# Mixture-of-experts routing: the map of tiles to tokens in bf16 parts, and two pieces of weight splitting moved to GpSimd

## The reference, cut to what matters

```python
logits = x @ w_gate                                # x: 2048 x 256
logits = SOFTCAP * jnp.tanh(logits / SOFTCAP)
probs = jax.nn.softmax(logits, axis=-1)
_, idx = jax.lax.top_k(probs, TOPK)                # TOPK = 2, E = 8
mask = jax.nn.one_hot(idx, E, dtype=probs.dtype).sum(-2)
weights = probs * mask
out = jnp.zeros_like(x)
for e in range(E):
    h = jax.nn.silu(x @ w1[e]) * (x @ w3[e])       # 256 x 512 each
    out = out + h @ w2[e] * weights[:, e:e + 1]    # 512 x 256
return out.reshape(orig_shape)
```

## Time and profile before

| | us |
|---|---|
| median of 3 runs | 1409.47 |
| lowest and highest run | 1405.94, 1411.13 |
| profiled execution, whole | 1412.31 |
| its span, first to last instruction | 1410.6 |

### The profile page before, as it was taken

The page is one execution under the profiler, slowest core; times in us unless marked ns, Lnnn a source line. Parts: engine busy times, 40 slices in busy tenths (PEclk is TensorE's granted clock), DMA queues, the critical chain, the costliest instruction groups (busy, mean ns, idle before and its releaser), DMA issues. The chain is left out here.

```text
span 1410.6 us, 28961 instructions
## 1 busy us (share of the span) xinstructions
PE 1322.5 (94%) x8611; PEld 1103.6 (78%) x8611; DVE 1084.0 (77%) x2711; ACT 955.8 (68%) x3247; POOL 917.4 (65%) x1109
## 2 busy tenths in 40 slices
PE   9999988897799999999999999999999978999991
PEld 4445666664599999999999999999999856899891
DVE  4899768896688888888888888888889856444443
ACT  3997457775488888888888878878778845323321
POOL 3996237774278787787887767767767824455542
PEclk9999999997999999999999999999999998999996
DMA  9421110000102002012020020010100257677764
GB/s 343 156 109 71 36 46 2 1 2 1 60 1 91 1 1 91 1 39 72 24 104 7 2 91 1 32 60 2 46 1 31 76 208 262 144 165 164 169 153 134
DMA packets 55164, 105.89 MB, mean 75 GB/s; under 512 B 5052, under 2 KB 33668, under 8 KB 52708
## 3 DMA queue, kind: packets, MB, share of 16 engines
q1 hardware_dynamic: 46100, 84.90, 17.5%
q0 software_dynamic: 7488, 10.23, 4.6%
q10 hardware_dynamic: 1424, 8.91, 1.5%
HBM read 75.58 MB, written 28.44 MB: 74 GB/s over the span
## 5 line engine op out<-in xcount | busy, mean ns | idle before, releaser
L1937 ACT ACTIVATE pr_<-ps,neg_ 128x128 f32<-128x128 f32 x512 | 181.0, 366 | 64.1 <-DVE neg_ L2131 64.1
L2024 POOL TENSOR_TENSOR rstd<-var,half 128x6 f32<-128x6 f32 x128 | 172.5, 1347 | 10.0
L1963 ACT ACTIVATE y<-ps,invsm 128x128 bf16<-128x128 f32 x512 | 146.2, 373 | 42.0 <-PE ps L1842 25.9
L2035 POOL TENSOR_TENSOR z<-t,m 128x512 fp32r<-128x512 bf16 x128 | 148.7, 1162 | 4.9 <-DVE t L2157 4.9
L1812 PE MATMUL ps<-qkt 128*128 128x128 f32 x1024 | 138.3, 278 | 2.2 <-ACT qkt L1929 2.1
L1853 PE MATMUL ps<-phi,z 128*128 128x256 f32 x512 | 138.1, 303 | 1.0 <-POOL z L2035 1.0
L2019 POOL TENSOR_TENSOR var<-stat,deps 128x6 f32<-128x6 f32 x128 | 26.1, 204 | 171.1 <-DVE stat L2096 171.0
L1812 PEld LDWEIGHTS ps<-qkt 128*128 128x128 f32 x1024 | 129.0, 191 | 6.9 <-ACT qkt L1921 2.7
L2028 POOL TENSOR_TENSOR pr_<-pr_,rec_ 128x512 f32<-128x512 f32 x128 | 132.8, 1038 | 2.0 <-DVE rec_ L2138 2.0
L1853 PE MATMUL ps<-plo,z 128*128 128x256 f32 x512 | 127.6, 280 | 0.0
L2613 POOL DMA_INDIRECT sums<-f_ys,f_ids x39 | 61.8, 1583 | 91.6 <-DMA sums<-f_ys,f_ids 74.8
(11 more groups left out here) (374 smaller groups left out, 4240.9 us busy)
## 6 DMA issues: line engine op xcount, KB each, us to landing
f_w_low<-w_low SPq DMA_DIRECT2D x39, 512.0 KB, 3.8
centred<-raw_weights ACTq DMA_DIRECT2D x8, 1024.0 KB, 3.9
w_low<-w_dram SPq DMA_DIRECT2D x8, 1024.0 KB, 11.7
aw_st<-centred SPq DMA_DIRECT2D x7, 1024.0 KB, 6.3
raw_weights<-wself_dram SPq DMA_DIRECT2D x4, 1024.0 KB, 13.8
raw_weights<-wcross_dram SPq DMA_DIRECT2D x4, 1024.0 KB, 14.5
w_rest<-w_dram SPq DMA_DIRECT2D x8, 512.0 KB, 4.0
w_high<-w_top SPq DMA_DIRECT2D x8, 512.0 KB, 2.7
```

The source lines that it names most:

```text
L1937: ins = act.activation(pr[:, u.par, h, :], bS[:, h * S:(h + 1) * S], ACT.Exp, bias=neg[:, u.par, h:h + 1], accum_out=tot[:, u.par, h:h + 1])
L1963: ins = act.activation(y[:, u.par, h * S:(h + 1) * S], bO[:, h * S:(h + 1) * S], ACT.Copy, scale=invsm[:, head:head + 1])
L2024: pool.tensor_tensor(rstd[:, u.par, 0:6], v, half[:, :], ALU.pow).then_inc(s_rstd, 1)
L2035: pool.tensor_tensor(z[:, u.par, :], t[:, u.par, :], m[:, u.par, :], ALU.subtract).then_inc(s_z, 1)
```

## The change

1. **The map in bf16.** Tile numbers, lane numbers, `at_tile` and `at_lane` are bf16, in which these small whole numbers are exact. The token's number is split: `first` (128 times the tile of tokens less 2048) and `behind` (partition less lane). `ids_of` holds both as 2 x 39 columns. VectorE makes `at_tile` for all 32 pairs in one operation and its product with `first` in another; GpSimd makes the product with `behind`, in 4 parts. All inputs lie in SBUF now.
2. **The shares in a second map.** Each share is cut into three bf16 parts that add up to it exactly (four small operations on GpSimd). VectorE multiplies them with `at_tile` (3 x 39 columns, 8 pairs at a time) behind `ids`, and 32 further TensorE products add them up in another bank. VectorE sums the three results to `weight`.
3. **The pieces.** TensorE subtracts pieces 0, 2, 4 and 5 (before 0, 2, 3 and 7), the banks of piece 4 between the groups of the map, those of piece 5 around the second map. GpSimd subtracts pieces 1 and 3 (`split_low_by_pool`), VectorE 6 and 7 (before 1, 4, 5 and 6). ScalarE alternates `split_high` and `keep` in halves.
4. **Waits.** The first gather waits for `ids` alone. The loads of `f_w_low` wait also for the second map.

```diff
-WARM_UNITS, WARM_PRODUCTS, WARM_AT_END, BY_PE = 4, (3, 4), 15, (0, 2, 3, 7)
+WARM_UNITS, WARM_PRODUCTS, WARM_AT_END, BY_PE = 4, (3, 4), 15, (0, 2, 4, 5)
+BY_POOL = (1, 3)
...
+    def split_low_by_pool(self, pool, q):
+        i, e = self.place(q)
+        pool.wait_ge(self.s_hi, q + 1)
+        pool.tensor_tensor(self.low[:, i, e, :], self.low[:, i, e, :].bitcast(F32),
+                           self.high[:, i, e, :].bitcast(F32), ALU.subtract).then_inc(self.s_lo_pool, 1)
...
                 sp.wait_ge(s_own, 1)
-                sp.wait_ge(s_ids, 2)
+                sp.wait_ge(s_ids, 1)
+                sp.wait_ge(s_shares_map, CHUNKS)
...
                 subtract(2)
...
+                for c in range(CHUNKS):
+                    map_ids(c)
+                    if c < CHUNKS - 1:
+                        subtract(4, range(c, c + 1))
+                subtract(4, range(CHUNKS - 1, PIECE * CB))
+                subtract(5, range(0, 2))
+                map_shares(0)
+                map_shares(1)
+                subtract(5, range(2, PIECE * CB))
+                map_shares(2)
+                map_shares(3)
...
                 experts.split_high(act, 1)
-                keep(0)
+                keep(0, early)
                 experts.split_high(act, 2)
+                keep(0, late)
                 experts.split_high(act, 3)
-                keep(2)
-                for q in range(4, UP_PIECES):
-                    experts.split_high(act, q)
-                keep(3)
-                keep(7)
+                keep(2, early)
+                experts.split_high(act, 4)
+                keep(2, late)
+                experts.split_high(act, 5)
+                keep(4)
+                experts.split_high(act, 6)
+                keep(5, early)
+                experts.split_high(act, 7)
+                keep(5, late)
...
+                experts.split_low_by_pool(pool, 1)
+                pool.wait_ge(s_mask, 1)
+                pool.tensor_copy(part[:, :, :, 0], best[:, :, :]).then_inc(s_part, 1)
+                pool.wait_ge(s_part, 1)
+                pool.tensor_tensor(rest[:, :, :], best[:, :, :], part[:, :, :, 0], ALU.subtract).then_inc(s_part, 1)
...
+                experts.split_low_by_pool(pool, 3)
+                pool.wait_ge(s_at_tile, 1)
+                pool.wait_ge(s_behind, 1)
+                for c in range(CHUNKS):
+                    pool.tensor_tensor(ids_of[:, c, :, 1, :], at_tile[:, c, :, :], across(behind, c, NT), ALU.mult
+                                       ).then_inc(s_behind_ids, 1)
...
+                dve.tensor_tensor(pairs(at_tile), tile_row[:, :].unsqueeze(1).to_broadcast([P, 2 * B, NT]), each(tile_code, NT),
+                                  ALU.is_equal).then_inc(s_at_tile, 1)
+                dve.wait_ge(s_at_tile, 1)
+                dve.wait_ge(s_first, 1)
+                dve.tensor_tensor(ids_of[:, :, :, 0, :].rearrange("p c n t -> p (c n) t"), pairs(at_tile), each(first, NT), ALU.mult
+                                  ).then_inc(s_first_ids, 1)
...
+                for c in range(CHUNKS):
+                    dve.tensor_tensor(at_lane[:, c, :, :], lane_row[:, :].unsqueeze(1).to_broadcast([P, CHUNK, P]),
+                                      across(lane_code, c, P), ALU.is_equal).then_inc(s_pairs, 1)
+                dve.wait_ge(s_map, CHUNKS)
+                link(dve.tensor_scalar(weight[:, :], ids_ps[:, 0:NT], empty[:, 0:1], None, ALU.add))
+                dve.tensor_tensor(ids[:, :], ids_ps[:, NT:2 * NT], weight[:, :], ALU.add).then_inc(s_ids, 1)
+                dve.wait_ge(s_part, 4)
...
+                share(0)
+                share(1)
+                owner_of_tiles()
                 experts.split_low(dve, 6)
+                share(2)
+                share(3)
+                experts.split_low(dve, 7)
```

More of the change, by code:

```diff
@@ L2331, in moe_layer @@
         tile_of = sbuf(ctx, "f_tile_of", [P, 2, B], F32)
-        lane_of = sbuf(ctx, "f_lane_of", [P, 2, B], F32)
-        token = sbuf(ctx, "f_token", [P, 2, B], F32)
-        token_i = sbuf(ctx, "f_token_i", [P, B], I32)
+        tile_code, lane_code, behind = (sbuf(ctx, "f_" + n, [P, 2, B], BF16) for n in ("tile_code", "lane_code", "behind"))
+        first_i, first = sbuf(ctx, "f_first_i", [P, 2, B], I32), sbuf(ctx, "f_first", [P, 2, B], BF16)
+        place_i, place = sbuf(ctx, "f_place_i", [P, 1], I32), sbuf(ctx, "f_place", [P, 1], F32)
+        rest = sbuf(ctx, "f_rest", [P, 2, B], F32)
+        part = sbuf(ctx, "f_part", [P, 2, B, 3], BF16)
         minus = sbuf(ctx, "f_minus", [P, P], F32R)
@@ L2344, in moe_layer @@
         (s_xh, s_cst, s_token, s_th, s_d, s_ex, s_mask, s_cnt, s_own, s_pairs, s_map, s_ids, s_xt, s_xe, s_up, s_si, s_mu, s_ht,
-         s_he, s_y, s_ye, s_go, s_minus, s_diff, s_left, s_link, s_at_tile, s_values) = (sem("f_" + n) for n in (
+         s_he, s_y, s_ye, s_go, s_minus, s_diff, s_left, s_link, s_at_tile, s_first, s_behind, s_behind_ids, s_first_ids, s_part, s_shares, s_shares_map) = (sem("f_" + n) for n in (
              "xh", "cst", "token", "th", "d", "ex", "mask", "cnt", "own", "pairs", "map", "ids", "xt", "xe", "up", "si", "mu",
-             "ht", "he", "y", "ye", "go", "minus", "diff", "left", "link", "at_tile", "values"))
+             "ht", "he", "y", "ye", "go", "minus", "diff", "left", "link", "at_tile", "first", "behind", "behind_ids", "first_ids", "part", "shares", "shares_map"))
         stats = sbuf(ctx, "f_stats", [P, B, 6], F32)
@@ L2424, in _, with subtract @@
             def _(pe):
-                def subtract(q):
+                def subtract(q, banks=range(PIECE * CB)):
                     pe.wait_ge(experts.s_hi, q + 1)
-                    for at, (i, e, c) in chunks(q):
+                    for at, (i, e, c) in chunks(q)[banks.start:banks.stop]:
                         if at >= len(turns):
@@ L2661, in _ @@
                 dve.wait_ge(s_mask, 1)
[L2662 to L2665 removed]
+                dve.wait_ge(s_token, 2)
+                dve.tensor_copy(first[:, :, :], first_i[:, :, :]).then_inc(s_first, 1)
+                link(dve.tensor_copy(place[:, :], place_i[:, :]))
+                link(dve.tensor_scalar(empty[:, :], place[:, :], float(TOK), None, ALU.add))
                 dve.wait_ge(s_cnt, 1)
@@ L2698, in _ @@
-                dve.wait_ge(s_values, 4 * B // CHUNK)
-                experts.split_low(dve, 1)
-                dve.wait_ge(s_map, 2 * B // CHUNK)
-                dve.tensor_scalar(ids[:, :], bH[:, 0:NT], empty[:, 0:1], None, ALU.add).then_inc(s_ids, 1)
-                dve.tensor_copy(weight[:, :], bH[:, NT:2 * NT]).then_inc(s_ids, 1)
-                link(dve.tensor_tensor(past[:, :, :], tile_no[:, :].unsqueeze(2).to_broadcast([P, NT + 1, E]),
-                                       end[:, :].unsqueeze(1).to_broadcast([P, NT + 1, E]), ALU.is_gt))
@@ L2705, in _ @@
-                link(dve.tensor_reduce(owner[:, :], past[:, :, :], AX.X, ALU.add))
-                dve.tensor_scalar(owners[:, :], owner[:, :], float(E - 1), None, ALU.min).then_inc(s_own, 1)
-                experts.split_low(dve, 4)
-                experts.split_low(dve, 5)
-                experts.split_low(dve, 6)
-                dve.wait_ge(s_ids, 2)
+                link(dve.tensor_scalar(tile_code[:, :, :], tile_of[:, :, :], -WHOLE, None, ALU.add))
+                link(dve.scalar_tensor_tensor(lane_code[:, :, :], tile_code[:, :, :], -float(P), row[:, :, :], ALU.mult, ALU.add))
@@ new lines, in _, with owner_of_tiles @@
+                dve.tensor_scalar(behind[:, :, :], lane_code[:, :, :], -1.0, place[:, 0:1], ALU.mult, ALU.add).then_inc(s_behind, 1)
+                def owner_of_tiles():
+                    link(dve.tensor_tensor(past[:, :, :], tile_no[:, :].unsqueeze(2).to_broadcast([P, NT + 1, E]),
+                                           end[:, :].unsqueeze(1).to_broadcast([P, NT + 1, E]), ALU.is_gt))
+                    link(dve.tensor_reduce(owner[:, :], past[:, :, :], AX.X, ALU.add))
+                    dve.tensor_scalar(owners[:, :], owner[:, :], float(E - 1), None, ALU.min).then_inc(s_own, 1)
@@ new lines, in _, with share @@
+                dve.wait_ge(s_part, 4)
+                def share(c):
+                    if c >= 2:
+                        dve.wait_ge(s_shares_map, c - 1)
+                    dve.tensor_tensor(shares[:, c % 2, :, :, :], at_tile[:, c, :, :].unsqueeze(2).to_broadcast([P, CHUNK, 3, NT]),
+                                      part[:, c // 2, c % 2 * CHUNK:c % 2 * CHUNK + CHUNK, :].unsqueeze(3).to_broadcast([P, CHUNK, 3, NT]),
+                                      ALU.mult).then_inc(s_shares, 1)
@@ L2712, in low_x @@
+                dve.wait_ge(s_ids, 1)
                 def low_x(u):
```

91 lines of the change are left out of this document (47 added, 44 removed).

## The result

The changed kernel takes 1418.95 us in the median of four runs (1418.74 to 1420.67), the kernel before beside it 1407.70 (1405.30 to 1411.13). The ratio is 1.0078, with a 95% interval of 1.0054 to 1.0101: slower by some 11 us. The forecast was 1417.5 us. The profiled execution of the changed kernel took 1420.67 us with a span of 1418.8, the one of before 1412.31 with 1410.6: 8.2 us between the spans, where the prediction's sum was 8.0. As the experiments show, that agreement is partly luck.

The account below looks back on a forecast made before the run. The prediction saw a race to the first up product between TensorE's queue and VectorE's routing. 8.6 + 2.8 - 3.3 + 0.3 - 0.4 = +8.0 us on the median 1409.47 gave 1417.5 us, 8-in-10 range 1406 to 1424.

Parts of the forecast that it names:

- Part 1: Routing on VectorE: two GpSimd pieces of up weights hold it at the shared port, +4.1 and +4.5, sum 8.6 us.
- the second small operation for the ids: Between the map and the first up product: one more small operation for ids, +0.3 us.
- rival B: VectorE's map and share operations: stall is there, but bf16 with a broadcast runs two a cycle; +4.2, 1413.7 us; chance 0.12.
- Part 2: New map on VectorE and GpSimd up to its first TensorE product: 4.9 us instead of 2.09, +2.8 us.
- Part 3: Map on TensorE: 32 bf16 products in four groups with three banks between, 8.7 us instead of 12.0, -3.3 us.
- during the map the granted clock is 0.50: TensorE during the old map: read from the profile as standing at the lower level of 1.2 GHz.
- Part 4: From ids to first up product: VectorE's row of 11.7 us ends last, against 12.1 before, -0.4 us.
- Nothing in the loop takes up a shift: Expert loop and adds: both keep one pace, 4.81 and 4.82 us, so earlier gains or losses reach the end.
- Rival A: VectorE beside the GpSimd pieces: it is not held up; 1406.4 to 1408.2 us, not slower; chance 0.12.
- Rival C: TensorE in map and shares: stays at the lower clock level; +12.7, 1422.2 us, more if it lasts; chance 0.12.
- Rival D: Second GpSimd piece: slips past the routing, so the stall costs 5 to 6 us; 1414 to 1415 us; chance 0.09.
- the profiled execution lies 2.84 above the median; the same difference on the median: Whole time: the profiled 1412.31 us lies above the three-run median 1409.47, so 1420.3 becomes 1417.5 us.

Follow-up runs that it names:

- `a_kept_warm`: Changed kernel with filler products on TensorE, 56 ahead of the map and 20 ahead of the first up product; 1427.11 us, 1.0105 of before.
- both directions: Changed kernel without its two GpSimd subtractions, 1412.84 us; kernel before with piece 1 moved from VectorE to GpSimd, 1411.33 us.
- `b_again`: The kernel before, unchanged, run once more for a second profile; 1405.35 us in one run.
- `a_pieces_by_tensor`: Changed kernel with pieces 1 and 3 on TensorE and ScalarE instead of GpSimd; 1411.38 us, 1.0021 of before.

## Why the prediction held, point by point

In times from `f_minus`, the prediction's marks were 21.6 for at_tile, 36.1 for the ids and 47.5 for the first up product; measured 21.04, 33.54 and 45.01.

- **Part 1**, +8.6 forecast, +8.07 measured (at_tile 12.97 before, 21.04 after). Right in mechanism, place and size: 4.5 us for a piece (4.54 and 4.53), VectorE rows of 4.23 and 4.27. The Trainium skill's rule ("SBUF — State Buffer", section "Who interferes with whom") is borne out for operations of 2048 elements: VectorE waits for the whole instruction. It held in the kernel before as well (4.19).
- **Parts 2 and 3** with the second small operation for the ids, together -0.2 forecast, -1.65 measured (at_tile to ids 14.15 before, 12.50 after). The bf16 comparison over a broadcast took 1.45 us, so rival B is out, and with it the reading that two elements a cycle might hold there; the Trainium skill ("VectorE: DVE Perf Modes", section "What auto-detection actually checks") agrees. Part 2, up to TensorE's first product, came at +2.59 (4.68 us against 2.09) where +2.8 was forecast. Part 3 with the second operation came at -4.24 (7.82 against 12.06) where -3.0 was forecast: a map group had been put at 0.92 from a transpose and took 0.47 to 0.74, and a group of at_lane beside a product of GpSimd came every 1.67 us, where 1.22 + 0.71 had been added up (and 1.22 alone for at_lane). The reading "during the map the granted clock is 0.50" leaves out that it was 1.00 until 1171.0.
- **Part 4** without that operation, -0.4 forecast, -0.93 measured (12.40 and 11.47). VectorE's row is what ends last, as said; from the ids ready (1187.04) to the first up product (1198.31) it was 11.3 us where 11.7 had been added up.
- So the first up product was forecast at +8.0 and came at +5.49.
- **"Nothing in the loop takes up a shift"** failed twice, by terms that stood in no sum. The first tile ran at the lower clock, where TensorE now waits 2.48 us for `f_xlo` behind the first transposes (1.36 before): +1.50. With fillers in that wait the tile took 8.94 us again (`a_kept_warm`). And the loop's pace changed with the tiles' addresses: +2.42. The prediction had named that as what would make it wrong. The two together with -1.19 from the stage's start and the end take the place of the missing 2.5: 5.49 + 2.73 = 8.22 against 8.0. The sum was right by terms that offset each other.
- **Rival A** is refuted by both directions. Rival C is half right: the clock was at the lower level for the first half of the map (two groups of 0.68 and 0.74 us) and again, unforeseen, at the first tile. Rival D didn't come: the second piece met the scan at once.
- **The base.** The prediction's whole picture of the map, 12.02 us mostly at the lower clock, is most likely that of one group of runs. Against such a run the change costs 8.8 us from `f_minus` on, against the other kind (`b_again`) 265.52 - 250.06 = 15.5. The measured 11 us is a mean over a mixture. The step "the profiled execution lies 2.84 above the median; the same difference on the median" took this for noise. Luck helps here too: by the medians the change cost 1418.95 - 1407.70 = 11.25 us where the sum had 8.0, and 1417.5 came within 1.5 us because it stood on 1409.47, the median of the first three runs, and not on 1407.70, that of four. Nor does the new map gain anything against the other kind: from at_tile to the ids it takes 12.50 us, and 1178.93 - 1168.55 = 10.38 in `a_pieces_by_tensor` with TensorE at the upper clock throughout, where the f32 map of `b_again` takes 1176.20 - 1166.56 = 9.64 from its first VectorE operation. The 7.42 us on TensorE lay almost wholly beside VectorE's and GpSimd's work (6.75 and 4.64 us busy from 1168 to 1176).

## What to carry to other kernels

Before giving GpSimd a long operation on two SBUF inputs because it is idle, look what VectorE does in that time: if it is a chain of small operations with two SBUF inputs, the chain pays the whole length of the piece, and another engine may take it for less (here TensorE with ScalarE). Where TensorE stands idle for a microsecond or two ahead of a stretch that is on the path, a second profile of the same kernel is worth more than a closer reading of the first, and ten small fillers were worth more here (4 us) than the new map. And a change that allocates tiles changes places: compare the pace of untouched loops before anything else is explained.

## What the runs showed of the hardware

- TensorE's clock in one and the same kernel: the map fell to 1.2 GHz after 2 us (0.50 from 1171 on, 12.02 us in all) in one profile and stayed at 2.4 GHz (1.00, 7.42 us) in another, where the idle time ahead was 1.44 and 1.34 us. Ten filler products gave 7.42 us in the profile and a single group of 12 runs.
- Where large tiles lie in SBUF moved the pace of products that don't read them: 4.813, 4.833 or 4.880 us for a tile, constant through the loop. The cause is open.
- VectorE and GpSimd take turns by the instruction on SBUF operands: a VectorE operation of 0.29 us took 4.23 beside a GpSimd one of 4.54, and 128x1024 bf16 took 1.67 us beside GpSimd's 128x312 products and in 1.22 without.
- Eight bf16 products of 78 columns start 0.29 us ahead of the next instruction at the upper clock (1184.24 to 1184.53 in `a_kept_warm`), some 36 ns each; an f32 product of this shape takes 7.42 / 32 = 232 ns.
